# A two-layer kernel on one core: the planner's table of task lengths and hand-over delays is replaced

## The reference, cut to what matters

```
# layer 0, on xn = layernorm(x)
m  = mamba(xn)                       # in_proj, conv of 4 taps, silu, dt/B/C projections, softplus
     h = exp(delta*A)*h + delta*B*u  # 512 channels x 16 states, scanned over 1024 tokens
     y = sum_n C_n*h_n + D*u ; y*silu(res) ; out_proj
f  = gelu(m @ w1.T + b1) @ w2.T + b2 # 256 -> 1024 -> 256
x  = x + normalised(m + f) + weights*(gelu_tanh(xn @ e1) @ e2)   # 256 -> 2048 -> 256, first batch only
# layer 1, on xn = layernorm(x)
attn = causal softmax attention, 16 heads of 16
mem  = exterior products of projected lines, squared incidence with decay, a sigmoid gate
x  = x + (attn + gate*mem_val) @ out_w + out_b + gelu(xn @ (W1 + s*m1)) @ (W2 + s*m2)
```

## Time and profile before

| what | value |
|---|---|
| three runs | 3908.34 us median (3906.81 to 3918.66) |
| the profiled execution | 3907.57 us, its span 3905.8 us |
| granted TensorE clock, mean | 0.972 |
| TensorE matmul busy | 3610.2 us, 92% |
| VectorE busy | 3178.4 us, 81% |
| ScalarE busy | 2659.1 us, 68% |
| GpSimd busy | 2288.1 us, 59% |

### The profile page before, as it was taken

The page is one execution under the profiler, slowest core; times in us unless marked ns, Lnnn a source line. Parts: engine busy times, 40 slices in busy tenths (PEclk is TensorE's granted clock), DMA queues, the critical chain, the costliest instruction groups (busy, mean ns, idle before and its releaser), DMA issues.

```text
span 3905.8 us, 63544 instructions
## 1 busy us (share of the span) xinstructions
PE 3610.2 (92%) x20512; PEld 2387.7 (61%) x20512; DVE 3178.4 (81%) x6108; ACT 2659.1 (68%) x4049; POOL 2288.1 (59%) x1788
## 2 busy tenths in 40 slices
PE   7999999999999999999798999999999998999998
PEld 3666566655556565656565666666566666656665
DVE  3788999998999999998957687786868778686874
ACT  6877878787787878877534657566575656657565
POOL 4687898898999899999814142332414233241421
PEclk9999999999999999999897999999999999999999
DMA  4345444454544555554522123232322323232220
GB/s 155 126 155 162 154 156 157 161 165 151 163 161 153 159 164 171 162 166 144 184 74 90 52 58 97 72 100 67 99 65 69 93 68 104 67 94 64 73 80 26
DMA packets 253340, 456.88 MB, mean 117 GB/s; under 512 B 26116, under 2 KB 80852, under 8 KB 250196
## 3 DMA queue, kind: packets, MB, share of 16 engines
q1 hardware_dynamic: 253012, 452.82, 37.1%
HBM read 381.07 MB, written 69.21 MB: 115 GB/s over the span
## 4 chain that ended last, share of the span: by engine, by line
PE 46%; DVE 13%; ACT 9%; issue 8%; POOL 1%; DVEq 0%; ACTq 0%; POOLq 0%
PE ps L1495 6%; PE ps L1608 5%; PE ps L1600 5%; PE ps L1476 4%; PE ps L1458 3%; DVE ps L2013 3%; PE ps L1360 3%; PE ps L1410 2%; PE ps L1529 2%; PE ps L1370 2%; DVE ps L2036 2%; ACT L1625 2%; PE ps L1535 2%; ACT h L1625 2%; ACT exps L1625 2%
## 5 line engine op out<-in xcount | busy, mean ns | idle before, releaser
L2270 POOL TENSOR_TENSOR drive<-du,b_wide 128x1024 f32<-128x1024 f32 x512 | 1202.0, 2363 | 204.3 <-DVE held L2013 122.1
L2304 POOL TENSOR_SCALAR_AFFINE_SELECT exps<-exps 128x256 f32<-128x256 f32 x512 | 204.1, 413 | 1000.5 <-ACT exps L1625 1000.0
L1625 ACT ACTIVATE ps<-delta,neg_a 128x512 f32<-128x512 f32 x1024 | 681.7, 685 | 146.2 <-DVE heavy L1991 132.2
L1625 ACT ACTIVATE exps<-ps 128x1024 f32<-128x1024 f32 (+1 forms) x640 | 596.5, 938 | 255.2 <-PE ps L1476 249.2
L2036 DVE CUSTOM_DVE_ANT_0 ps<-ps,later 128x512 f32<-128x512 f32 (+3 forms) x1024 | 474.7, 518 | 90.6 <-PE ps L1458 88.6
L1410 PEld LDWEIGHTS ps<-p_all,heavy 128*128 128x128 f32 x3072 | 361.9, 144 | 246.5 <-DVE heavy L1991 124.8
L1410 PE MATMUL ps<-p_all,heavy 128*128 128x128 f32 x3072 | 439.9, 280 | 76.2 <-DVE heavy L1991 69.2
L1991 DVE TENSOR_TENSOR heavy<-c_wide,ps 128x512 f32<-128x512 f32 x704 | 467.6, 670 | 8.2 <-issue 4.1
L2013 DVE TENSOR_TENSOR_SCAN ps<-ps,carry,drive 128x512 f32<-128x512 f32 x352 | 441.5, 1272 | 32.8 <-ACT ps L1625 32.5
L2013 DVE TENSOR_TENSOR_SCAN ps<-ps,drive 128x512 f32<-128x512 f32 x352 | 420.4, 1214 | 48.3 <-ACT ps L1625 46.0
L2039 DVE TENSOR_REDUCE smax<-ps 128x2 f32<-128x1024 f32 x256 | 312.1, 1220 | 112.0 <-PE ps L1458 109.3
(11 more groups left out here) (211 smaller groups left out, 7158.7 us busy)
## 6 DMA issues: line engine op xcount, KB each, us to landing
b_wide<-bc_dram SPq DMA_DIRECT2D x512, 256.0 KB, 3.4
c_wide<-bc_dram SPq DMA_DIRECT2D x512, 256.0 KB, 3.5
stacks<-parts SPq DMA_DIRECT2D x192, 256.0 KB, 2.5
qs<-stacks SPq DMA_DIRECT2D x128, 192.0 KB
ks<-stacks SPq DMA_DIRECT2D x128, 192.0 KB, 4.3
x_row<-in_x SPq DMA_DIRECT2D x14, 1024.0 KB, 7.9
resid<-mix SPq DMA_DIRECT2D x9, 1024.0 KB, 5.3
x_row<-resid SPq DMA_DIRECT2D x9, 1024.0 KB, 5.4
```

What stands on the lines that cost most here:

```text
L1625: return nc.scalar.activation(out_, in_, func, **kw)
L2270: G.tensor_tensor(drive[:, g % DRIVE_SLOTS, :, :], du[:, e, :, :], wide(b_wide[:, g % B_SLOTS, :], MD), ALU.mult).then_inc(driven, 1)
```

## The change

Only the planner's numbers change. Lengths of most kinds are replaced in `LENGTH0`, `EMPTY0`, `LENGTH`, `EMPTY_A`, `EMPTY_V`, in `scores_length` and in the numbers written into the `add` calls. A new table LATE gives each engine's delay until others feel its end, 0.2 us for TensorE, 0.18 ScalarE, 0.16 VectorE, 0.12 GpSimd and 0.06 SyncE; before, it was 0.06 for all where a call names none. A PSUM bank is now free at the end of its drain plus the draining engine's delay. Ticks, `LEAD0`, `LEAD`, `LAG`, `SPANS`, `TURN`, `FIRST`, `DRIFT`, `SHORT`, `RUN`, the pace model and every instruction that a task issues stay as they are. The kernel therefore issues the same instructions, in another order within each engine and with other bank numbers.

```
-LENGTH0 = {"xt": 0.46, "xm": 1.74, "cv": 3.46, "res": 1.74, "xd": 3.46, "dl": 0.88, "yt": 0.46, "m": 3.46, "h": 1.74,
-           "o": 4.0, "mu": 0.4, "var": 0.4, "mh": 1.74, "mo": 3.5}
-EMPTY0 = {"xt": 0.66, "xm": 0.66, "cv": 0.66, "res": 0.66, "xd": 0.6, "dl": 0.68, "yt": 0.62, "m": 0.62, "h": 0.66,
-          "o": 0.42, "mu": 0.4, "var": 0.2, "mh": 0.62, "mo": 0.45}
+LATE = {"p": 0.2, "a": 0.18, "v": 0.16, "g": 0.12, "s": 0.06}
+LENGTH0 = {"xt": 0.44, "xm": 1.72, "cv": 3.44, "res": 1.72, "xd": 3.46, "dl": 1.05, "yt": 0.44, "m": 3.46, "h": 1.72,
+           "o": 3.68, "mu": 0.2, "var": 0.2, "mh": 1.72, "mo": 3.46}
+EMPTY0 = {"xt": 0.48, "xm": 0.49, "cv": 0.58, "res": 0.49, "xd": 0.48, "dl": 0.59, "yt": 0.48, "m": 0.48, "h": 0.58,
+          "o": 0.33, "mu": 0.14, "var": 0.1, "mh": 0.49, "mo": 0.38}
...
-    def add(engine, unit, length, tick, *after, late=0.06):
+    def add(engine, unit, length, tick, *after, late=None):
...
+                                    LATE[engine] if late is None else late)
...
-            add("g", ("drive", g), 2.36, tick - 6, ("s", "b", g), only(j, ("g", "du", j, e)),
+            add("g", ("drive", g), 2.32, tick - 6, ("s", "b", g), only(j, ("g", "du", j, e)),
...
-                add("g", ("weigh", g), 2.6, tick + 2, ("v", "scan", MD * g + MD - 1), ("s", "c", g))
+                add("g", ("weigh", g), 2.35, tick + 2, ("v", "scan", MD * g + MD - 1), ("s", "c", g))
...
-                add("v", ("scan", k), 1.2 if j % NC else 1.13, k, ("a", "decay", k), ("g", "drive", g),
+                add("v", ("scan", k), 1.175 if j % NC else 1.13, k, ("a", "decay", k), ("g", "drive", g),
...
-                    add("v", ("weigh", k), 0.6, k + 1.5, ("v", "scan", k), ("s", "c", g),
+                    add("v", ("weigh", k), 0.59, k + 1.5, ("v", "scan", k), ("s", "c", g),
...
-                    add("p", ("add", piece), 0.47, k + LEAD0["add"], ("v", "weigh", k))
+                    add("p", ("add", piece), 0.44, k + LEAD0["add"], ("v", "weigh", k))
...
-LENGTH = {"xt": 0.44, "qk": 1.30, "pa": 1.18, "pb": 1.30, "lt": 0.44, "jw": 0.89, "fw": 0.44, "fr": 0.44, "ms": 0.44,
-          "zt": 0.44, "wo": 1.72, "e1": 0.23, "e2": 0.23, "f1": 1.30, "o": 3.44}
-EMPTY_A = {"xt": 0.61, "qk": 0.69, "pa": 0.55, "pb": 0.24, "lt": 0.6, "jw": 0.49, "zt": 0.6, "f1": 0.8, "mt": 0.27}
-EMPTY_V = {"xt": 0.62, "qk": 0.75, "pa": 0.6, "pb": 0.43, "fw": 1.42, "fr": 0.75, "ms": 0.22, "e1": 0.75, "e2": 0.75, "o": 0.42,
-           "wo": 0.68, "mt": 0.28, "ot": 1.1}
+LENGTH = {"xt": 0.44, "qk": 1.40, "pa": 1.28, "pb": 1.40, "lt": 0.44, "jw": 0.89, "fw": 0.44, "fr": 0.44, "ms": 0.44,
+          "zt": 0.44, "wo": 1.72, "e1": 0.23, "e2": 0.23, "f1": 1.46, "o": 3.44}
+EMPTY_A = {"xt": 0.48, "qk": 0.59, "pa": 0.33, "pb": 0.13, "lt": 0.5, "jw": 0.44, "zt": 0.49, "f1": 0.73, "mt": 0.25}
+EMPTY_V = {"xt": 0.6, "qk": 0.66, "pa": 0.42, "pb": 0.34, "fw": 1.36, "fr": 0.67, "ms": 0.11, "e1": 0.66, "e2": 0.66, "o": 0.34,
+           "wo": 0.61, "mt": 0.25, "ot": 0.96}
...
-    return 0.02 + sum(max(0.107, width_of(*one) / 2400) for one in unit)
+    return sum(max(0.12, width_of(*one) / 2230) for one in unit)
...
-                add("v", ("lines", b, t), 1.1, place["pb", b, t], ("g", "outer", b, t))
+                add("v", ("lines", b, t), 0.6, place["pb", b, t], ("g", "outer", b, t))
...
-                    bank_free[bank] = end + 0.06
+                    bank_free[bank] = end + LATE[e]
```

More of the change, by code:

```diff
@@ L219, in layer0_tasks @@
     tasks, before = {}, {}
-    def add(engine, unit, length, tick, *after, late=0.06):
+    def add(engine, unit, length, tick, *after, late=None):
         kind = (engine, unit[0])
-        tasks[(engine,) + unit] = (length, tick, [a for a in after + (before.get(kind),) if a], late)
+        tasks[(engine,) + unit] = (length, tick, [a for a in after + (before.get(kind),) if a],
+                                    LATE[engine] if late is None else late)
         before[kind] = (engine,) + unit
@@ L254, in layer0_tasks @@
                     skip = piece_of(j, e, 0, d)
-                    add("a", ("skip", q, d), 0.66, tick - 4, ("a", "silu_x", j) if j else None,
+                    add("a", ("skip", q, d), 0.61, tick - 4, ("a", "silu_x", j) if j else None,
                         only(skip >= W_SLOTS, ("p", "add", skip - W_SLOTS)))
-                    add("p", ("add", skip), 0.47, tick - 2 + LEAD0["add"], ("a", "skip", q, d), only(q, ("v", "gate", q - 1)))
+                    add("p", ("add", skip), 0.44, tick - 2 + LEAD0["add"], ("a", "skip", q, d), only(q, ("v", "gate", q - 1)))
                 add("a", ("decay", k), 0.63 + (0.2 if last >= 0 and last // STEPS % NC == 0 else 0), k - 4,
@@ L329, in layer0_tasks @@
         if kind == "cv" and last == MI - 1:
-            add("a", ("silu_x", j), 4.5, start + 2, ("a",) + unit)
+            add("a", ("silu_x", j), 4.4, start + 2, ("a",) + unit)
         elif kind == "res" and last == TC - 1:
-            add("a", ("silu_g", j), 4.5, start + 2, ("a",) + unit)
+            add("a", ("silu_g", j), 4.4, start + 2, ("a",) + unit)
         elif kind == "xd":
@@ L335, in layer0_tasks @@
         elif kind == "dl" and last == MI - 1:
-            add("a", ("soft", j), 4.5, start + 2, ("a",) + unit)
+            add("a", ("soft", j), 4.4, start + 2, ("a",) + unit)
         elif kind == "h" and last == MF - 1:
-            add("a", ("gelu", j), 6.2, start + 2, ("a",) + unit)
+            add("a", ("gelu", j), 6.1, start + 2, ("a",) + unit)
         elif kind == "o":
-            add("v", ("spread", j, last), 0.42, start + 3, ("v",) + unit, ("v", "gather", j // NC - 1))
+            add("v", ("spread", j, last), 0.335, start + 3, ("v",) + unit, ("v", "gather", j // NC - 1))
             if j % NC == NC - 1 and last == TC - 1:
@@ L350, in layer0_tasks @@
             for i in range(TC):
[L351 removed]
+                add("g", ("join", j, i), 1.23, start + 8, ("a", "centre", j), ("s", "again", j))
             add("s", ("keep", j), 0.5, start + 9, ("g", "join", j, TC - 1), late=7.0)
@@ L502, in pair @@
             add("p", ("sm", g, n), scores_length(unit, max_width), tick, ("s", "stack", g) if n == 0 else None)
-            add("v", ("sm", g, n), sum(1.16 if it // TC > ch else 0.22 + max_width(it, ch) / 485 for it, ch in unit)
-                + (0.09 if n == len(MAX_UNITS) - 1 else 0), tick, ("p", "sm", g, n))
+            add("v", ("sm", g, n), sum(1.135 if it // TC > ch else 0.21 + max_width(it, ch) / 485 for it, ch in unit)
+                + (0.26 if n == len(MAX_UNITS) - 1 else 0), tick, ("p", "sm", g, n))
         place["mt", g] = first + TICKS - LEAD
@@ L545, in layer1_tasks @@
         for i in range(NT // 2):
-            add("v", ("stats", b, i), 0.9, start - 18, ("s", "fetch", b))
-        add("v", ("spread", b), 1.5, start - 14, ("v", "stats", b, NT // 2 - 1))
+            add("v", ("stats", b, i), 0.66, start - 18, ("s", "fetch", b))
+        add("v", ("spread", b), 0.87, start - 14, ("v", "stats", b, NT // 2 - 1))
         add("a", ("deviation", b), 2.8, start - 13, ("v", "spread", b))
@@ L550, in layer1_tasks @@
         for i in range(NT // 2):
-            add("v", ("normal", b, i), 0.9, start - 11, ("v", "inverse", b))
+            add("v", ("normal", b, i), 0.66, start - 11, ("v", "inverse", b))
         add("a", ("split", b), 0.33, start - 10, ("v", "normal", b, 0), ("s", "rows", b - 1, 1) if b else None)
@@ L579, in layer1_tasks @@
             free = ("p", "fr", b, c - 1, FCH - 1) if c else None
-            add("g", ("feat_r", b, c), 4.4, at, ("v", "unit", b, c), free)
-            add("g", ("feat_w", b, c), 4.4, at, ("a", "jw", b, c), free)
+            add("g", ("feat_r", b, c), 4.15, at, ("v", "unit", b, c), free)
+            add("g", ("feat_w", b, c), 4.14, at, ("a", "jw", b, c), free)
             for ch in range(FCH):
@@ L586, in layer1_tasks @@
             for ch in range(1, FCH):
-                add("g", ("sum", b, c, ch), 1.27, place["fr", b, c, ch] + 1, ("v", "fr", b, c, ch))
+                add("g", ("sum", b, c, ch), 1.22, place["fr", b, c, ch] + 1, ("v", "fr", b, c, ch))
             for i in range(2):
@@ L590, in layer1_tasks @@
             add("a", ("logistic", b, c), 0.5, place["ms", b, c, 1], ("v", "ms", b, c, 1))
-            add("v", ("gate", b, c), 2.9, place["ms", b, c, 1], ("a", "logistic", b, c), ("v", "pb", b, TC * c + TC - 1))
+            add("v", ("gate", b, c), 2.6, place["ms", b, c, 1], ("a", "logistic", b, c), ("v", "pb", b, TC * c + TC - 1))
         for kind in ("e1", "e2"):
```

40 lines of the change are left out of this document (20 added, 20 removed).

## The result

The changed kernel takes 3972.64 us (median of 4 runs, 3969.98 to 3984.07) against 3911.08 us: a ratio of 1.0174, 95% interval 1.0155 to 1.0193. It is slower, by some 62 to 68 us, where 3893 us and a gain were forecast; the time lies outside the range. The profiled execution is the slowest of the four, 3984.07 us with a span of 3982.4 us, so sums made on its trace come out some 10 us above the medians.

The account below looks back on a forecast made before the run. TensorE alone was taken to bound layer 1, three nearly equal engines layer 0. The profiled 3907.6 us less 10 (layer 1) and 5 (layer 0) gave 3892.6, as a median 3893 us; range 3862 to 3945, likeliest case 3870 to 3896.

Parts of the forecast that it names:

- What bounds: TensorE alone bounds layer 1, idling 105 us; in layer 0 three engines lie within 4 points of each other.
- 10 and 5 us: Expected savings from truer delays: 10 us in layer 1 and 5 us in layer 0.
- Delays: The old list thought results usable about 0.1 to 0.14 us early; layer 1: 104 TensorE waits x 0.12 us = 12.5 us.
- The sign that I gave for being right: From 2100 to 3850 us, TensorE's waits for exps and maxima fall from 104 and 69.5 us by a tenth or more.
- VectorE's cover: In layer 1 VectorE idles 435 of 1750 us behind TensorE, so errors in its booked lengths cost nothing.
- such a contention: GpSimd contends with VectorE's two-input SBUF instructions, so no fixed `lines` length is right; costed at nothing.
- More turns: Rival, chance 0.17: in layer 1 more scores units stand alone or between turns, costing 30 us: 3925 to 3930 us.
- the rival's 32 us: Layer 0 rival, chance 0.16: VectorE stands about 2 us more in each of 16 halves: 3935 to 3940 us.

Follow-up runs that it names:

- 5 ns: The kernel before with its one delay of 0.06 us set to 0.065 us everywhere: 3969.28 us, ratio 1.0160.
- the two searched orders: Due places searched anew, in the changed kernel (3889.76 us, ratio 0.9963) and in the kernel before with its old numbers (3910.30 us, ratio 1.0010).
- the filled run: The changed kernel, order untouched, with matmuls of overwritten result added where TensorE stands ahead of a half clock: 3969.04 us, ratio 1.0162.
- delays x 0.8: The changed kernel with each delay at 0.8 of its value: 3947.67 us, ratio 1.0113.
- LEAD 17: LEAD 17 for 18, nothing else: in the kernel before 3971.98 us (layer 0 passage); in the changed kernel with searched places 3942.56 us (list of four orders).
- retuned: The changed kernel with new lengths and delays, but due places and weights searched for the shortest booked order: 3889.76 us, ratio 0.9963.

## Why the prediction was wrong, point by point

**What bounds.** TensorE bounds layer 1, as said, and what a new order can save lies in the idle times. The step that failed is the next one: that what it can *cost* lies near that too. The forecast summed 0.12 us a wait, 10 and 5 us in all, as if the order stayed and only its small stalls closed. The list is greedy, and one choice moved re-arranges the rest of a batch, the same way in each of eight. Apart from the two whose places were searched and the one that kept the old numbers in layer 1, every order that was tried has 1987 to 2024 us in layer 1, against 1950 before. The new numbers' merit, whatever it is, is smaller than this spread. A step of 5 ns cost as much as the whole change (63 us), and the two searched orders under either table lie 20 us apart: what was lost is the order, not the 10 + 5 us of stalls. The text named it as what could make it wrong ("two orders of the same work can differ by more than the delays that I count"), and gave it no size.

**Delays.** The kind of wait they were to close did shrink, from 37 with 19.4 us to 18 with 8.2 at the second scores, 11 us and not the 37 x 0.12 = 4.4 of the sum. The term said nothing of the new waits, which gave it back. It was also summed too evenly: 0.12 us is ScalarE's share, and only 67 of the 104 waits are for ScalarE; with 0.06 for the 24 on GpSimd and 0.10 for the 13 on VectorE it is 10.8 us and not 12.5. The sign that I gave for being right, these seven kinds falling by a tenth, did not come: they are 102 with 77.5 us. (They hold the waits for `xn` too; those for exps and maxima alone were 95 with 60.6.)

**VectorE's cover.** I costed VectorE's new lengths at nothing, since it idles 435 of 1750 us. That is a mean over a batch. In the memory part it is busy 3.37 of 3.40 and 3.56 of 3.60 us and TensorE waits for it: no cover there. The wait for the tile `lines`, 7 with 6.9 us, is for the end of the `unit` task, whose length went from 2.65 to 2.29. Before, it took 2.29 us at the place shown (2971.03 to 2973.32); in the changed order it takes 2.97 (3005.20 to 3008.17), since GpSimd's `outer` now comes first. My text had such a contention, but for the three instructions of the `lines` task (1.1 to 0.6), and put it under the same cover. That either length is at fault was not tried alone.

**The clock.** It has no term in the sum. By the filled run it carries most of the 48 us by which the same matmuls are busy longer; the 20 us of idle time are not its doing, and in the 5 ns run the idle part is the larger one. One order at two clocks shows its price as well: the four runs of "delays x 0.8" go from 3934 us at a mean clock of 0.971 to 3966 at 0.957. The stretches of the earlier trace rows had it: 0.98 in layer 1, and 0.90 where TensorE idles more.

**More turns.** My test for this rival was that busy time rises with unchanged counts. It did, but the clock does the same. Taken together, both scores groups' matmuls went from 557 to 563 us, 6 us, so lone scores are not where the 48 us are. A test that two mechanisms pass tells nothing between them.

**Layer 0.** 9 us longer instead of 5 shorter; the rival's 32 us did not come. One execution each does not settle the 9 us: with the order of before in layer 0 (all of it with LEAD 17, all but two units with the new numbers in layer 1 only) it ended at 1956, 1959 and 1966 us. The run with the new numbers in layer 0 only, 13 us slower by its medians, says that some of it is real. The lengths alone make it 32 us longer (1988), the delays alone 3 us shorter (1953). The unit lengths that I compared with the trace were those of undisturbed places; whether the new ones are too short on average was not tried.

**What stays open.** Whether a truer table pays. For it: one search with each table, 3890 against 3910 us, and four orders under the new table (retuned, LEAD 17, delays x 0.8, changed) of which the one that the list books shortest is the fastest. Against it: the new table books the order of before as the worse one. One draw of each is not a proof, and that the new table is truer was checked at a few rows only. Nor is it shown which choice of the list, in which place, the 5 ns decide, or what removing the clash of `outer` and the multiply alone would give.

## What to carry to other kernels

When a change goes through a planner, plan and run its neighbours first: a step that means nothing (5 ns, one tick) shows how far orders scatter, and that scatter, here 53 to 68 us in 3908 for three such steps, belongs in the forecast before any sum of stalls. Part of it can be read without a run, in the length that the list books for the neighbour under the same numbers. An order that was better than its neighbours can lose by an edit that makes the numbers truer, until its places are searched again; so judge new planner numbers only after such a search, with a control that searches under the old ones. And look for cover in the stage where the edit acts: VectorE's 25% of idle time over the layer was 1% in the part that mattered.

## What the runs showed of the hardware

In the place shown, two idle gaps of 0.99 and 0.46 us within 3 us, behind one of 0.64 us a little earlier, stand ahead of 10 us at 1.2 GHz, in which TensorE was busy all the time; in the kernel before, where the gaps were 0.43 and 0.22 us, the clock stayed at 2.4 GHz. Of seven batches with the same two gaps six had 0.50 to 0.55 and one 0.83, so the gaps alone do not fix what follows. Over six batches the growth of TensorE's busy time, 42 us, is three times the growth of its idle time, 14 us. Transposes of the identity in idle places raised layer 1's clock from 0.94 to 0.97 and did not make the kernel faster clear of noise.

VectorE's multiply of two SBUF tiles (128x768, 1.1 us) and GpSimd's (128x512, 1.1 us) that overlapped took 1.8 us for whichever started second, by as little as 0.1 us: GpSimd in seven batches before, VectorE in seven batches after.
